# LoRA adapters on 4096 tokens, one core: A loaded by ScalarE's queue in 512-byte runs, B by SyncE's, and A's preparation moved ahead of B's table copies and of the first tiles

## What is computed

```python
# x [64, 64, 1024] f32, ids [64] in 3..7, A [8, 1024, 16], B [8, 16, 1024]
Bx  = einsum('bni,bri->bnr', x, B[ids])     # down: 1024 -> rank 16
out = einsum('bnr,bor->bno', Bx, A[ids])    # up: rank 16 -> 1024
return x + out                              # SCALING is 1
```

## Time and profile before

| | |
|---|---|
| median of 3 runs | 96.18 us (95.92 to 96.72) |
| profiled execution, its own time | 96.29 us |
| its span, first to last instruction | 94.4 us |
| busy PE / VectorE / ScalarE / GpSimd | 81.5 / 58.4 / 53.1 / 67.1 us |
| DMA | 34.83 MB, 11202 packets, 369 GB/s over the span |
| mean granted TensorE clock | 0.945 |

### The profile page before, as it was taken

One profiled execution on the slowest core, in us unless ns is written; L12 is line 12 of the kernel. 1 busy time (PEld: TensorE's weight loads), 2 busy tenths in 40 slices (PEclk: granted clock), 3 DMA queues, 4 the chain that ended last, 5 costly groups with the idle time before them and its releaser, 6 DMA issues.

```text
span 94.4 us, 3723 instructions
## 1 busy us (share of the span) xinstructions
PE 81.5 (86%) x1472; PEld 64.5 (68%) x1472; DVE 58.4 (62%) x105; ACT 53.1 (56%) x138; POOL 67.1 (71%) x152
## 2 busy tenths in 40 slices
PE   3994999999999999899999999999989999652800
PEld 3993998787786768587877787777767877440400
DVE  0009541219696949396969677685857695949760
ACT  2219687985747475657667676757556757110000
POOL 6003906379798999979797979797979798986000
PEclk9999999999999999999999999999999999975555
DMA  1999999999999999999999999999999998664676
GB/s 19 305 294 394 419 417 408 408 408 412 401 413 406 408 403 403 410 412 403 408 413 408 419 403 415 417 412 415 417 410 419 410 380 327 271 266 198 247 318 252
DMA packets 11202, 34.83 MB, mean 369 GB/s; under 512 B 2866, under 2 KB 2866, under 8 KB 11186
## 3 DMA queue, kind: packets, MB, share of 16 engines
q1 hardware_dynamic: 11040, 34.08, 91.7%
q10 hardware_dynamic: 146, 0.52, 1.6%
HBM read 17.83 MB, written 16.78 MB: 367 GB/s over the span
## 4 chain that ended last, share of the span: by engine, by line
PE 69%; POOL 9%; DMA 7%; issue 5%; DVE 4%; POOLq 2%; DVEq 1%
PE t_bank L221 31%; PE bx_bank L234 18%; PE y_banks L254 16%; POOL a_duo L162 7%; DMA x_all<-in_A 7%; PE y_banks L212 4%; DVE x_all L363 1%; DVE x_all L341 1%; POOL b_duo L151 1%; DVEq L43 1%; DVE x_all L338 1%; DVE x_all L344 1%; POOL bx_parts L169 1%; POOLq L43 0%; POOLq L162 0%
## 5 line engine op out<-in xcount | busy, mean ns | idle before, releaser
L363 DVE TENSOR_TENSOR x_all<-y_banks,x_all 128x1024 f32<-128x1024 f32 x32 | 39.1, 1224 | 18.7 <-PE y_banks L254 18.2
L301 ACT COPY x_t<-t_bank 128x512 f32<-128x512 f32 x64 | 34.4, 591 | 19.5 <-PE t_bank L221 19.5
L162 POOL CAST a_duo<-a_table 128x512 fp32r x64 | 36.6, 609 | 3.4 <-ACT a_table L306 3.2
L221 PE MATMUL t_bank<-ident,x_all 128*128 128x128 f32 x256 | 34.9, 279 | 1.3 <-DMA x_all<-in_x 1.2
L221 PEld LDWEIGHTS t_bank<-ident,x_all 128*128 128x128 f32 x256 | 27.5, 141 | 7.8 <-issue 4.9
L151 POOL COPY b_duo<-b_table 128x256 f32 x64 | 23.2, 403 | 11.1 <-ACT b_table L287 6.2
L254 PE MATMUL y_banks<-a_duo,bx_parts 64*128 64x512 f32 x128 | 20.8, 445 | 4.0 <-POOL bx_parts L169 3.5
L234 PE MATMUL bx_bank<-x_t,b_duo 128*32 128x64 f32 x1024 | 21.7, 222 | 1.1 <-issue 0.6
L234 PEld LDWEIGHTS bx_bank<-x_t,b_duo 128*32 128x32 f32 x1024 | 16.2, 109 | 7.1 <-issue 6.2
L254 PEld LDWEIGHTS y_banks<-a_duo,bx_parts 64*128 64x128 f32 x128 | 12.0, 197 | 7.5 <-issue 3.5
L355 DVE TENSOR_TENSOR bx_parts<-bx_bank,bx_parts 32x64 fp32r<-32x64 f32 x64 | 14.0, 219 | 4.8 <-ACT bx_parts L316 3.7
(11 more groups left out here) (13 smaller groups left out, 7.4 us busy)
## 6 DMA issues: line engine op xcount, KB each, us to landing
out_y<-x_all SPq DMA_DIRECT2D x32, 512.0 KB, 12.4
x_all<-in_x SPq DMA_DIRECT2D x15, 1024.0 KB, 18.8
x_all<-in_x SPq DMA_DIRECT2D x2, 512.0 KB, 6.0
x_all<-in_B ACTq DMA_DIRECT2D x1, 512.0 KB, 4.1
x_all<-in_A SPq DMA_DIRECT2D x1, 512.0 KB, 6.2
id_row<-in_ids ACTq DMA_DIRECT2D x1, 0.2 KB
```

Of the source, the lines that this page charges most:

```text
L162: last = nc.gpsimd.tensor_copy(a_duo[duo % 2][:, k, :], a_table[:, bass.ds(adapters[k] * BANK, BANK)])
L221: last = nc.tensor.transpose(t_bank[unit % 2][:, c * P:(c + 1) * P], x_all[:, 2 * duo + tile, at:at + P], ident[:, :])
L301: nc.scalar.copy(x_t[duo % 2][:, half * HALF:(half + 1) * HALF, tile, :], t_bank[unit % 2][:, :].rearrange("p (c n) -> p c n", c=HALF)).th ...
L363: nc.vector.tensor_tensor(here, y_banks[tile][:, :], here, ALU.add).then_inc(y_drained, 1)
```

## The change

- A goes to ScalarE's queue, ahead of the ids, and B to SyncE's, ahead of x.
- A is read in 1024 runs of 512 bytes: partition p now holds the eight output features 8p + 4h + j of each adapter.
- Column (h, p, j) of the product is then feature 8p + 4h + j, so the add reads `y_banks` in runs of four elements from its two banks in turn; x is read and written in natural order.
- ScalarE does its three instructions on A before the two copies to `b_table`.
- PE transposes adapters 0 to 3 first, then all four units of duo 0, then adapters 4 to 7. Before it was two units, four adapters, two units, four adapters. ScalarE's copies follow that order.

```diff
@@ block.sync
-            sp.dma_start(a_nat.rearrange("p a h j r -> p (a h) (j r)"),
-                         a_in.rearrange("a (h p j) r -> p (a h) (j r)", h=HALVES, j=J)).then_inc(a_loaded, 16)
+            sp.dma_start(b_nat, b_in.rearrange("a r i -> (a r) i")).then_inc(b_loaded, 16)
@@ block.tensor
-            transpose_unit(0, 0)
-            transpose_unit(0, 1)
             for a in range(A_BANKS):
                 a_unit(a)
-            transpose_unit(0, 2)
-            transpose_unit(0, 3)
+            for unit in range(UNITS):
+                transpose_unit(0, unit)
             for a in range(A_BANKS, ADAPTERS):
                 a_unit(a)
@@ block.scalar
-            act.dma_start(b_nat, b_in.rearrange("a r i -> (a r) i")).then_inc(b_loaded, 16)
+            act.dma_start(a_nat.rearrange("p a h j r -> p a (h j r)"),
+                          a_in.rearrange("a (p h j) r -> p a (h j r)", h=HALVES, j=J)).then_inc(a_loaded, 16)
             act.dma_start(id_row[:, :], ids.rearrange("(o s) -> o s", o=1)).then_inc(ids_loaded, 16)
+
+            act.wait_ge(a_loaded, 16)
+            for h in range(HALVES):
+                nc.scalar.copy(a_rounded(h, 1, 0), a_nat[:, :, h, :, :]).then_inc(a_high_act, 1)
+            act.wait_ge(a_rest_dve, 1)
+            nc.scalar.copy(a_rounded(0, 1, 1), a_part(0, 0, 1)).then_inc(a_rest_act, 1)
 
             for unit in range(B_UNITS):
...
-            act.wait_ge(a_loaded, 16)
-            for h in range(HALVES):
-                nc.scalar.copy(a_rounded(h, 1, 0), a_nat[:, :, h, :, :]).then_inc(a_high_act, 1)
-            act.wait_ge(a_rest_dve, 1)
-            nc.scalar.copy(a_rounded(0, 1, 1), a_part(0, 0, 1)).then_inc(a_rest_act, 1)
...
-            copy_x(0, 0)
-            copy_x(0, 1)
             copy_a(A_BY_ACT[0])
             copy_a(A_BY_ACT[1])
-            copy_x(0, 2)
-            copy_x(0, 3)
+            for unit in range(UNITS):
+                copy_x(0, unit)
@@ block.vector
-                here = x_all[:, 2 * duo + tile, :]
-                nc.vector.tensor_tensor(here, y_banks[tile][:, :], here, ALU.add).then_inc(y_drained, 1)
+                here = x_all[:, 2 * duo + tile, :].rearrange("n (p h j) -> n p h j", h=HALVES, j=J)
+                product = y_banks[tile][:, :].rearrange("n (h p j) -> n p h j", h=HALVES, j=J)
+                nc.vector.tensor_tensor(here, product, here, ALU.add).then_inc(y_drained, 1)
```

## The result

The changed kernel takes 100.47 us in the median of 5 runs (100.13 to 101.24), against 96.42 for the kernel before in the same series: ratio 1.045, 95% interval 1.041 to 1.050. It is slower by 4.3 us by the ratio, where 11.1 were forecast. The profiled execution took 101.24 us, with a span of 99.5 and a mean granted clock of 0.91. The other four had spans of 98.2 to 98.4 and clocks of 0.926 to 0.939, so the profile shows a little more of the slow clock than the median has. Some executions of any kernel come out over 1.5% above its fastest one: ratios leave these out, medians hold them.

What follows compares the result with a forecast made beforehand. The prediction took the engines, a train of 16 duos whose departure the head sets, as the bound. It summed 9.3 us for the later departure and 1.8 for the clock to +11.1, giving 107.3 us, eight-in-ten range 101 to 109.

Steps and rivals of the forecast that it cites:

- The bound and the method: Engines, not DMA, set the end; a microsecond lost or won ahead of the loop comes out at the end.
- the loop's departure: Start of duo 1's first units on PE: 14.05 us before, forecast 23.4 us after, +9.3 us.
- A's landing less 5.6: General form at the head: the loop's shift in us equals A's landing time less 5.6.
- One packet from each queue in turn: DMA at the head: each of A's 64 packets per engine waits for a 4096-byte packet; 11.5 us, landing 14.9.
- The sharing by bytes: Rival in DMA: an engine takes up to 4096 bytes of small packets per turn; A not late, 96.5 us; chance 0.07.
- the rule of whole packets: Skill page in DMA: an engine drains a packet of typically 9 to 17 descriptors before switching queues; supports a 0.07 rival.
- The head start: Rival in DMA: ScalarE's queue keeps its lead, A runs alone first; 97.6 to 105.8 us, middle 101; chance 0.15.
- The order: PE's head: four units in a row with ScalarE's copies; departure 5.8 us behind the first adapter instead of 4.40.
- The clock: PE after ten idle microseconds: first 16 transposes at 1.2 GHz, +1.8 us, bounds 0 and 2.3.
- The add: VectorE in the loop: reading two banks in runs of four costs 0; rival that it doubles, 119 us, chance 0.03.
- B, the ids and the loads of x: Loads at the head: their new places in the queues delay nothing that PE or GpSimd needs; cost 0.
- small "issue" pieces: PE: less traffic beside instruction fetches could save five pieces, about 1.1 us; counted at none, -1.1 as a bound.

Runs made afterwards that it cites:

- the first run: The kernel before with only A's 512-byte runs and the add that belongs to them: median 96.61 us, ratio 0.9954.
- experiment 7: The changed kernel with SyncE waiting for A's landing between B's load and x's: median 97.88 us, 4 runs, no ratio.
- the last run of experiment 8: The kernel before with 512-byte runs, early ScalarE splits, A, B, x in one queue, and PE order adapters, two units, adapters, two units: 96.68 us, ratio 1.0066.
- experiments 3 and 4: The kernel before with only the new PE and ScalarE order: 97.55 us; the changed kernel with 30 more transposes filling PE's idle time before A: 98.17 us.
- experiment 5: The changed kernel with A's load issued only when B has landed: 112.13 us, ratio 1.163.
- experiment 2: The kernel before with only the queues of A and B swapped, A still in 256-byte runs: 107.22 us, ratio 1.113.

## Why the prediction was wrong

**The bound and the method held.** In the ten kernels whose chain goes through the loop's departure (the two compared ones among them) it is 78.7 to 80.2 us from there to the end, so the end followed it within 1.5 us. In the three others (the first run, experiment 7, the last run of experiment 8) the chain of the loop runs over GpSimd, and it is 80.7 to 82.9 us by the timeline; two of these profiled executions are the slowest of theirs. The general form I gave, "A's landing less 5.6", was right: with the measured landing of 8.6 it gives +3.0, and the parts of the departure other than the clock are +1.63 for the landing, +1.50 for the order (as in experiments 3 and 4), and -0.07 from landing to first adapter, together 3.06.

**The step that failed** is in the DMA part: "SyncE's queue holds B and behind it 16 MB of x ..., and it does not run dry". It did, for a microsecond, right behind B, while A's load, issued ahead of x's, was served. I had read how the queues share when both are full, and took for granted that a queue with issued loads is full. Nothing in the trace of before spoke for that, as x stood behind A there. In the pause A moved 631 packets; only some 300 had to take turns, not 1024. That is the landing at 8.6 in place of 14.9, and 6.3 us of the departure. A's first packet was late too: none came before 3.25, where I had taken 2.6. Experiment 5 made the step true and was even slower than the forecast; experiment 2 shows the pause with A's packets doubled, and starvation behind it. Why the pause does not grow with A's packets stays open.

**One packet from each queue in turn** was right: 141 beside 139, 865 beside 863, 916 beside 920. Such counts alone would also fit groups of packets from each queue in turn. But in four stretches of about one turn each (0.18 to 0.19 us, from 5.60 to 6.35) A has 15, 15, 17 and 16 packets on the 16 engines. And when A's packets begin behind a full queue, in experiment 5 from 8.30 to 8.60, there are 13 of them, of 27 ns each (7.3% of 16 engines' time), beside 27 of x: had every engine served nine or more in a row, there would be over a hundred.

The sharing by bytes, and the rule of whole packets in the Trainium skill's page "DMA: Bandwidth & Descriptors" (Queues, rings and completion order), show in none of these traces, with runs of 256 or of 512 bytes.

**The head start** was the rival that came nearest, its middle at 101, but by another mechanism. A did not begin first: its first packets came after B's, and it ran alone behind B. That this middle lies near the 100.47 measured is luck. I had put 0.15 on it and the range's lower end at 101, half a microsecond too high.

**The order** was priced at +1.4 (0.87 for two units, 0.5 for the stall) and measured +1.50: right. **The clock** was priced at +1.8, with 2.3 as the upper bound and ten idle microseconds as the ground. It came after 3.6 idle ones, and was 2.43 in the profiled execution (19.70 - 11.21 = 8.49 us from first adapter to departure, against 6.06 with PE kept busy) and 2.3 between the medians: x's units 0 and 1 ran at 1.2 GHz too (1.72 us in place of 0.87). **The add** at nothing, and **B, the ids and the loads of x** at nothing, were right. Of the small "issue" pieces counted at zero with -1.1 as a bound, some may have come back: the stretch from departure to end is 0.4 us shorter. In the rival of sharing by bytes, the landing at 5.6 from which it decides asks for 34 ns a packet ((5.6 - 0.8 - 2.6) / 64), not 37; nothing else hangs on it.

## What to carry to other kernels

Before a load is moved to another queue, count packets per engine, not bytes: beside a stream of full packets each small one pays for a large one. Here one queue did best, with long runs: let it carry what is wanted first, in the order in which it is wanted, with the bulk behind it. A queue that is issued is not yet full, so look when its first packets come. And a wait in front of PE costs a second time where the clock falls in it: the same landing with PE kept busy was 2.3 us cheaper.

## What the hardware showed unexpectedly

- **The first packets of successive loads** are far apart at the start of a kernel. In the changed kernel A's first came after 3.2, though it was issued at 0.74 beside B, and x's came at about 5 though issued at 1.18; with twice as many packets for A they came no later. In experiment 5 A was issued at 4.39, behind several loads of SyncE, and its first packet came after 8.2; x's, with no load of A ahead of them, came before 4 (SyncE's queue moved 0.65 MB up to 4.00, of which 0.52 are B). This looks as if packets were prepared for one load after another, whichever queue it is on; that is my reading. Experiment 5 speaks for it, and the pause of experiment 2, no longer with twice the packets, limits it: preparing a load does not take time by its packets. No run settles it.
- **Run length when alone:** 277 GB/s in 256-byte packets, 342 in 512-byte ones (0.34 MB in the stretch 4.00 to 5.00 of experiment 7), 401 in 4096-byte ones. At 342, A alone would need 1.5 us, not the 1.3 of the prediction.
- **A late loop is shorter.** From departure to the end of the span it is 80.2 us before, 79.8 after, 78.7 in experiment 2 and 78.8 in experiment 5, which depart last. It is no strict order: the kernel that departs first (one queue, long runs) has 79.5. By the starts of GpSimd's gathers of A, the first steady periods take 4.41 to 4.43 us, as in the prediction. Then come periods of 4.6 to 4.9: eight before, up to 76 us; four after, up to 64; three in experiment 5, up to 61. Behind them it is 4.4 to 4.5 again. They end near where DMA falls from 410 GB/s (at about 76, 67 and 55 us), but they begin long after it is full. That the busy DMA is their cause is argued from their place alone.
